# Layer 3's depthwise convolution: planes padded to nine columns, shifted copies made by the loads, taps split by the vector engine

## What is computed

```python
def _L3_conv_ref(x, w, b):
    xp = jnp.pad(x, ((0, 0), (0, 0), (3, 3), (3, 3)), mode='reflect')
    out = jax.lax.conv_general_dilated(xp, w, window_strides=(1, 1), padding='VALID',
              dimension_numbers=('NCHW', 'OIHW', 'NCHW'), feature_group_count=192)
    return out + b[None, :, None, None]
...
x = x + _L3_conv_ref(_gn(x), L3_conv_w, L3_conv_b)
```

## Time and profile before

| | us |
|---|---|
| median of 3 runs | 2519.12 (2515.17 to 2522.4) |
| profiled execution | 2517.25 |
| its span, first to last instruction | 2515.5 |
| TensorE busy | 1945.1 (77%) |
| VectorE busy | 1287.4 (51%) |
| ScalarE busy | 804.7 (32%) |
| POOL busy | 870.2 (35%) |
| layer 3's block, from its first normalisation to the end | 2316.3 to 2515.5 |

### The profile page before, as it was taken

How to read it: one execution, slowest core, us unless ns; L and a number is a source line. 1 busy time by engine, 2 the same in 40 slices (tenths; PEclk the granted TensorE clock), 3 DMA queues, 4 the chain that set the end, 5 groups by cost and what they waited for, 6 DMA issues and landing times. The chain is left out here.

```text
span 2515.5 us, 36893 instructions
## 1 busy us (share of the span) xinstructions
PE 1945.1 (77%) x15660; PEld 1203.3 (48%) x15660; DVE 1287.4 (51%) x1313; ACT 804.7 (32%) x1269; POOL 870.2 (35%) x459
## 2 busy tenths in 40 slices
PE   3879779769999999999978768777777777774052
PEld 1577666667777777777734322222222222221031
DVE  6445444441111111111271166799999999988803
ACT  3445445440000000000122125633543533335410
POOL 3334233220000000000000040599899899983300
PEclk9889899889999999999988778899899979987555
DMA  7899999988131313130120040678688868863799
GB/s 197 249 311 314 316 292 304 296 257 241 59 118 59 118 60 118 60 118 1 43 59 11 0 139 21 156 197 219 171 213 216 209 175 213 218 179 90 224 215 294
DMA packets 195538, 424.51 MB, mean 169 GB/s; under 512 B 18733, under 2 KB 143661, under 8 KB 184717
## 3 DMA queue, kind: packets, MB, share of 16 engines
q1 hardware_dynamic: 182540, 414.81, 58.8%
q10 hardware_dynamic: 12832, 7.34, 1.1%
HBM read 299.33 MB, written 121.96 MB: 167 GB/s over the span
## 5 line engine op out<-in xcount | busy, mean ns | idle before, releaser
L743 PE MATMUL ps<-mem 128*128 128x288 f16 x5376 | 654.6, 287 | 14.4 <-DMA mem<-depthwise_out 14.4
L743 PEld LDWEIGHTS ps<-mem 128*128 128x128 f16 x5376 | 502.1, 98 | 152.9 <-issue 15.4
L1717 POOL TENSOR_TENSOR mem<-mem 128x1024 f32<-128x1024 f32 x192 | 465.7, 2444 | 45.3 <-ACT mem L1651 42.9
L1626 PE MATMUL ps<-mem 128*128 128x512 f32 x768 | 417.9, 676 | 39.1 <-POOL mem L1717 35.0
L1112 POOL TENSOR_TENSOR mem<-mem 128x1536 f16<-128x1536 f32 x16 | 50.8, 3180 | 940.3 <-ACT mem L1090 940.3
L533 PE MATMUL ps<-mem 56*96 56x240 f16 (+1 forms) x5184 | 308.2, 280 | 86.1 <-DMA mem<-base_phases 53.0
L533 PEld LDWEIGHTS ps<-mem 56*96 56x96 f16 x5184 | 297.7, 128 | 111.4 <-DMA mem<-base_phases 58.5
L786 DVE TENSOR_TENSOR mem<-ps,mem 128x128 f16<-128x128 f32 x64 | 18.7, 292 | 586.8 <-ACT mem L807 586.8
L1746 DVE TENSOR_TENSOR_SCAN mem<-mem,ps 128x1024 f32<-128x1024 f32 x132 | 307.8, 2332 | 18.2 <-issue 10.3
L646 DVE TENSOR_TENSOR mem<-ps,mem 96x1024 f16<-96x1024 f32 x144 | 175.3, 1220 | 217.9 <-ACT mem L578 217.9
L1626 PEld LDWEIGHTS ps<-mem 128*128 128x128 f32 x768 | 153.5, 213 | 242.9 <-issue 134.5
(11 more groups left out here) (202 smaller groups left out, 1915.4 us busy)
## 6 DMA issues: line engine op xcount, KB each, us to landing
mem<-l_bc SPq DMA_DIRECT2D x504, 256.0 KB, 4.5
depthwise_out<-mem SPq DMA_DIRECT2D x105, 512.0 KB, 9.4
mem<-depthwise_out SPq DMA_DIRECT2D x31, 1664.0 KB, 10.8
mem<-base_phases SPq DMA_DIRECT2D x72, 448.0 KB
base_phases<-mem SPq DMA_DIRECT2D x56, 512.0 KB, 9.9
mem<-in_wd SPq DMA_DIRECT2D x72, 336.0 KB
mem<-l_planes SPq DMA_DIRECT2D x48, 252.0 KB
mem<-in_x SPq DMA_DIRECT2D x4, 2048.0 KB, 13.6
```

The lines of the kernel that those rows point to most:

```text
L743: ins = nc.tensor.matmul(ps[:, 2 * (i % 2) + h, 0:HALF], d, pw[rows, wa, k, HALF * h:HALF * h + HALF], start=(k == 0 and n == 0), stop=(k ...
L1626: ins = nc.tensor.matmul(py[:, a, :], ident, hh[:, n % 4, 512 * a:512 * a + 512], start=(n % N == 0), stop=(n % N == N - 1))
L1717: nc.gpsimd.tensor_tensor(hh[:, n % 4, :], hh[:, n % 4, :], cs[:, n % 4, :], ALU.mult).then_inc(hc_pool, 1)
```

## The change

- A plane becomes 18 rows of 9 blocks and 2 elements more (164). The ninth column lies between the end of one row and the start of the next, so the phases that are shifted by one block are the same data one element further on. SBUF and DRAM hold only the 32 phases; the copies L1952 and L2013 go.
- A half window is loaded by three transfers (`load_windows`): 32 phases, then 12 rows of them one element later and 12 one element earlier. `planes_d` has the phase outermost, so a row of a half window is one run of 10.5 KB, and a tile is stored in pieces of 656 bytes. SP loads the halves t = 0, ACT the halves t = 1.
- Six column copies stay, into the ninth column; the mirrored rows are copied in twelve pieces; the values that nothing writes are cleared first (`clear`), and POOL clears one element at each end of a window.
- The taps' low parts are made by DVE: piece 0 after tile 1, pieces 1 to 3 after tile 2. `w32` and `win` no longer share memory. TensorE waits for piece n // 3 before batch n.
- SP loads windows 0 to 2 after the store of tile 1 and ahead of that of tile 2.

```diff
-PLANE = 18 * 8
+PLANE = 18 * 9 + 2
...
-        planes_d = nc.dram_tensor("l3_planes", [B, C, TAPROWS, 2 * PLANE], F16).ap()
+        planes_d = nc.dram_tensor("l3_planes", [PHASES, C, B, 2 * PLANE], F16).ap()
...
-    pl = ar.take16(2, TAPROWS * 2 * PLANE, dt=F16)
-    cv = pl.rearrange("p a n -> p (a n)").bitcast(F32)[:, 0:NT * HW].rearrange("p (t n) -> p t n", t=NT)
-    pl = pl.rearrange("p a (c r h n) -> p a c r h n", r=4, h=2, n=PLANE)
+    shared = ar.take(NT * HW)
+    cv = shared.rearrange("p (t n) -> p t n", t=NT)
+    pl = shared[:, 0:PHASES * 2 * PLANE].bitcast(F16).rearrange("p (a f r h n) -> p a f r h n", a=2, f=8, r=4, h=2)
     wh = ar.take16(2, NB3 * WC, dt=F16)
-    at = ar.at
     win = ar.take16(NW, BP, PITCH, dt=F16)
-    end = ar.at
-    ar.at = at
     w32 = [ar.take(3 * WC) for _ in range(2)]
...
-        return pl[:, t % 2, 0:8, r, a, 8:136]
+        return pl[:, t % 2, :, r, a, 0:18 * 9].rearrange("p f (y x) -> p f y x", x=9)[:, :, 1:17, 1:9]
...
+    def load_windows(eng, n, t):
+
+        last, c0 = BP * PITCH, CB * n + BP * t
+        src = planes_d[:, c0:c0 + BP].rearrange("f c b n -> f (c b n)")
+        dst = win[64 * t:64 * t + TAPROWS, n % NW].rearrange("f c n -> f (c n)")
+        eng.dma_start(dst[0:32], src).then_inc(win_in[n % NW], 16)
+        eng.dma_start(dst[32:44, 1:last], src[20:32, 0:last - 1]).then_inc(win_in[n % NW], 16)
+        eng.dma_start(dst[44:56, 0:last - 1], src[0:12, 1:last]).then_inc(win_in[n % NW], 16)
...
                     load_taps(sp, t + 2)
                 sp.wait_ge(rows_done, t + 1)
                 for p0, b, c0, n in pieces(t):
-                    sp.dma_start(planes_d[b, c0:c0 + n].rearrange("c f n -> c (f n)"),
-                                 pl[p0:p0 + n, t % 2].rearrange("p c r h n -> p (c r h n)")).then_inc(stored[t], 16)
-            sp.wait_ge(tap_hi, NPIECE)
-            sp.wait_ge(tap_lo, NPIECE)
-            sp.wait_ge(stored[0], used + 16)
-            sp.wait_ge(stored[1], used + 16)
-            for n in range(NB3):
-                if n >= NW:
-                    sp.wait_ge(conv_sum, n - NW + 1)
+                    sp.dma_start(planes_d[:, c0:c0 + n, b].rearrange("f c n -> c f n"),
+                                 pl[p0:p0 + n, t % 2].rearrange("p f r h n -> p (f r) (h n)")).then_inc(stored[t], 16)
+                if t == 1:
+                    sp.wait_ge(win_cleared, 2)
+                    sp.wait_ge(stored[0], used + 16)
+                    sp.wait_ge(stored[1], used + 16)
+                    for n in range(NW):
+                        load_windows(sp, n, 0)
+            for n in range(NW, NB3):
+                sp.wait_ge(conv_sum, n - NW + 1)
                 if CB * n == 128:
                     sp.wait_ge(stored[2], used + 32)
-                for t in range(2):
-                    for b in range(B):
-                        c0 = CB * n + BP * t
-                        sp.dma_start(win[64 * t:64 * t + TAPROWS, n % NW, :, 2 * PLANE * b:2 * PLANE * b + 2 * PLANE],
-                                     planes_d[b, c0:c0 + BP].rearrange("c f n -> f c n")).then_inc(win_in[n % NW], 16)
+                load_windows(sp, n, 0)
...
-                pe.wait_ge(win_in[n % NW], win_base[n % NW] + 64 * (n // NW + 1))
-                if n == 0:
-                    pe.wait_ge(tap_hi, NPIECE)
-                    pe.wait_ge(tap_lo, NPIECE)
+                pe.wait_ge(win_in[n % NW], win_base[n % NW] + 96 * (n // NW + 1))
+                if n % 3 == 0:
+                    pe.wait_ge(tap_hi, n // 3 + 1)
+                    pe.wait_ge(tap_lo, n // 3 + 1)
...
+                                    out = ps[M3 * j:M3 * j + M3, bank(n) + t, 256 * h:256 * h + 256].rearrange("p (b y x) -> p b y x", b=B, x=8)
+                                    ins = nc.tensor.matmul(out, taps_of(n, 4 * h + j, o, t, a), x[:, :, xa, 9 * o:9 * o + 144].rearrange("p b (y x) -> p b y x", x=9)[:, :, :, 1:9],
...
-            def shift_right(t):
-                k = t % 2
-                act.wait_ge(x_lo, 4 * (t + 1))
-                nc.scalar.copy(grid(pl[:, k, 8:11])[:, :, :, 1:8], grid(pl[:, k, 5:8])[:, :, :, 0:7]).then_inc(shifted, 1)
-
             normalise(0)
             taps(0)
-            for t in range(NT):
-                shift_right(t)
-                if t + 1 < NT:
-                    normalise(t + 1)
-                taps(t + 1)
+            normalise(1)
+            taps(1)
+            normalise(2)
+            act.wait_ge(win_cleared, 2)
+            act.wait_ge(stored[0], used + 16)
+            act.wait_ge(stored[1], used + 16)
+            for n in range(NW):
+                load_windows(act, n, 1)
+            taps(2)
+            taps(3)
+            act.wait_ge(x_lo, 4 * NT)
...
+                if n + NW < NB3:
+                    if CB * (n + NW) == 128:
+                        act.wait_ge(stored[2], used + 32)
+                    load_windows(act, n + NW, 1)
...
-            def taps(i):
-                pool.wait_ge(tap_hi, i + 1)
-                s = slice(3 * WC * i, 3 * WC * (i + 1))
-                q = slice(0, 64 + TAPROWS)
-                nc.gpsimd.tensor_tensor(wh[q, 1, s], w32[i % 2][q], wh[q, 0, s], ALU.subtract).then_inc(tap_lo, 1)
-
-            for i in range(NPIECE):
-                taps(i)
+            edge = win.rearrange("p a c n -> p a (c n)")
+            nc.gpsimd.memset(edge[:, :, 0:1], 0.0).then_inc(win_cleared, 1)
+            nc.gpsimd.memset(edge[:, :, BP * PITCH - 1:BP * PITCH], 0.0).then_inc(win_cleared, 1)
...
+            def pads(t):
+
+                def at(f, n):
+                    return pl[:, t % 2, f, :, :, n:n + 144].rearrange("p r h (y x) -> p r h y x", x=9)[:, :, :, :, 0]
+
+                for i in (1, 2, 3):
+                    V.tensor_copy(at(8 - i, 9), at(i, 10)).then_inc(columns, 1)
+                for i in (0, 1, 2):
+                    V.tensor_copy(at(i, 18), at(6 - i, 17)).then_inc(columns, 1)
...
-                k = t % 2
-                dve.wait_ge(shifted, 2 * (t + 1))
+                p = pl[:, t % 2]
                 dve.wait_ge(columns, 6 * (t + 1))
                 for r in range(1, 4):
-                    V.tensor_copy(pl[:, k, :, r, :, 0:8], pl[:, k, :, 4 - r, :, 8:16])
+                    V.tensor_copy(p[:, 3:8, r, :, 0:9], p[:, 3:8, 4 - r, :, 9:18])
+                    V.tensor_copy(p[:, 0:3, r, :, 1:10], p[:, 0:3, 4 - r, :, 10:19])
                 for r in range(3):
-                    ins = V.tensor_copy(pl[:, k, :, r, :, 136:144], pl[:, k, :, 2 - r, :, 128:136])
+                    V.tensor_copy(p[:, 3:8, r, :, 153:162], p[:, 3:8, 2 - r, :, 144:153])
+                    ins = V.tensor_copy(p[:, 0:3, r, :, 154:163], p[:, 0:3, 2 - r, :, 145:154])
                 ins.then_inc(rows_done, 1)
 
-            for k in range(2):
-                V.memset(pl[:, k, :, 0, :, 0:8], 0.0).then_inc(zeroed, 1)
-                V.memset(pl[:, k, :, 3, :, 136:144], 0.0).then_inc(zeroed, 1)
+            def taps(i):
+                dve.wait_ge(tap_hi, i + 1)
+                s, q = slice(3 * WC * i, 3 * WC * (i + 1)), slice(0, 64 + TAPROWS)
+                V.tensor_tensor(wh[q, 1, s], w32[i % 2][q], wh[q, 0, s], ALU.subtract).then_inc(tap_lo, 1)
+
+            def clear(k):
+
+                p = pl[:, k].rearrange("p f r h n -> p (f r h) n")
+                V.memset(p[:, :, 0:162].rearrange("p g (y x) -> p g y x", x=9)[:, :, :, 0:1], 0.0).then_inc(zeroed, 1)
+                V.memset(p[:, :, 162:164], 0.0).then_inc(zeroed, 1)
+                V.memset(pl[:, k, :, 0, :, 1:9], 0.0).then_inc(zeroed, 1)
+                V.memset(pl[:, k, :, 3, :, 154:162], 0.0).then_inc(zeroed, 1)
+
+            clear(0)
+            clear(1)
+            dve.wait_ge(zeroed, 8)
             for t in range(NT):
-                k = t % 2
                 if t == 2:
                     dve.wait_ge(stored[0], used + 16)
                 for r in range(4):
                     dve.wait_ge(x_norm, 4 * t + r + 1)
-                    V.tensor_copy(main_rows(t, r, 0), phase_rows(r)).then_inc(x_hi, 1)
+                    V.tensor_copy(main_rows(t, r, 0), flat(phase_rows(r))).then_inc(x_hi, 1)
                     dve.wait_ge(x_hi, 4 * t + r + 1)
-                    V.tensor_tensor(main_rows(t, r, 1), phase_rows(r), main_rows(t, r, 0), ALU.subtract).then_inc(x_lo, 1)
+                    V.tensor_tensor(main_rows(t, r, 1), flat(phase_rows(r)), main_rows(t, r, 0), ALU.subtract).then_inc(x_lo, 1)
                 dve.wait_ge(x_lo, 4 * t + 4)
-                V.tensor_copy(grid(pl[:, k, 11:14])[:, :, :, 0:7], grid(pl[:, k, 0:3])[:, :, :, 1:8]).then_inc(shifted, 1)
-                for i in range(3):
-                    V.tensor_copy(column(k, 8 + i, 0), column(k, 3 - i, 0)).then_inc(columns, 1)
-                    V.tensor_copy(column(k, 11 + i, 7), column(k, 6 - i, 7)).then_inc(columns, 1)
+                pads(t)
                 rows(t)
+                if t == 1:
```

(4 more changed lines are left out.)

11 lines of the change are left out of this document (2 added, 9 removed).

## The result

The changed kernel takes **2555.45 us** (median of 4 runs, 2551.64 to 2568.42), the kernel before 2519.40 beside it: the ratio is **1.0142**, with an interval of 1.0121 to 1.0164. It is 36 us slower. The forecast was 2511 with a range of 2497 to 2529, and 0.23 for slower.

A forecast was written before the change was run, and what follows sets the result against it. It took plane building, then window loads (6.5 us a batch) and instruction packets (5.94 us a burst) as bounds. TensorE would end at 2474 instead of 2481.6, -7.6 us: span 2508, median 2511, range 2497 to 2529.

The forecast's parts named there:

- Start of layer 3: ScalarE's first normalising step, taken at 2316.3 us as in the kernel before.
- Clearing: Eight VectorE memsets ahead of tile 0: 2.9 us, 0.8 of it seen, as VectorE waits for its first row anyway.
- Planes and casts: VectorE building planes: cast stays at 0.69 us, twelve row copies at 0.11 each; tile 1 done at 2341.3, not 2351.0.
- The stores' wait: SyncE's stores wait for taps' low parts: store 0 at 2344.4, store 1 at 2374, windows at 2389 instead of 2374.
- Stores: Plane stores in 656-byte pieces at 42 ns: 10.8 us each, plus 1 to 2 for completion and 3.3 for taps.
- Rival C: Plane stores: 656-byte pieces are slow, 62 to 65 ns each, giving 2527 us; chance 0.18.
- First windows: First window loads issued at 2389, 0.5 issue + 2 + 4.7 us; TensorE starts at 2396, 5 us earlier.
- The gap before batch 3: Store 2, 10.8 us, ahead of batch 3's half window in SyncE's queue: TensorE idles 5 us, batch 3 at 2420.
- Steady state: Last nine batches at 6.0 us each, from 2420 to 2474; windows and stores 6.6 at most, instruction packets 4.1 to 6.7.
- Tail: From last matmul to the end, eviction, store, load, add and output store: 33.9 us, as before.
- Rival D: Window halves don't overlap on two queues: 221 GB/s, 7.2 us a batch, 2522 us (2525 with slow first group); chance 0.15.

The follow-up runs named there:

- e16: e12 with SyncE's loads of the convolution's sums issued only after ScalarE's half of the last window load; 2498.71 us, ratio 0.9906.
- e10: The changed kernel, clearing only pads that nothing writes later (256 single elements a buffer instead of 1152); 2554.10 us.
- e17: The same kernel as e10, run again with five rounds; 2547.96 us, ratio 1.0097.
- e1: The changed kernel with SyncE's load of taps t + 2 issued after store t + 1 instead of ahead of store t; 2519.34 us, ratio 0.9996.
- e4: The changed kernel with the taps' low parts made by GpSimd again, SyncE's order as in the change; 2520.76 us, ratio 0.9999.
- e2: The changed kernel with all window loads in SyncE's queue, none in ScalarE's; 2555.18 us, ratio 1.0138.
- e3: The changed kernel with the eight clearing memsets made by GpSimd instead of VectorE; 2555.91 us, ratio 1.0144.
- e12: e5 with store 2 issued by GpSimd instead of SyncE; 2505.20 us, ratio 0.9937.
- e14: The same kernel as e5, run again with five rounds; 2510.56 us, ratio 0.9956.
- e9: e5 without the two 12-row loads of a half window from the fourth batch on (sums not valid); 2488.00 us, ratio 0.9866.
- e5: The changed kernel with small clearing and mended order: early stores ahead of tap loads, windows ahead of store 2, taps copied earlier; 2506.33 us, ratio 0.9939.
- e6: e5 with store 2 issued ahead of SyncE's first window loads instead of behind them; 2512.47 us, ratio 0.9954.

## Why the prediction was wrong

The wait that makes the kernel slower was named; what the forecast set against it did not come. It had 85 us from the first window's issue to the last matmul (2389 to 2474), where the kernel before takes 107.7. Measured: 119.8 (2402.0 to 2521.8). The windows, store 2 and the stored sums of that stretch are some 23 MB, so 85 us would have needed about 270 GB/s (an estimate from the sizes of the transfers); the two stretches above that cover most of it show 224 and 233, and the quickest kernel of the study, e16, took 96 us for it. **That is the step that failed: each transfer was priced by itself.** Store 2 was 10.8 us, a batch 6.0 where its own two terms made 6.6, and the sums that the first batches store beside store 2 were left out. By the steps of the prediction, against the profiled execution (span forecast 2508, measured 2554.5):

- **Start of layer 3:** +1.4 us, chance.
- **Clearing (wrong, +7.2):** put at 2.9 us, of which 0.8 seen, from a memset of 768 f32 elements. That row is of contiguous elements. 1152 single ones take 5.1 to 5.2 us, twice; e10 and e17 show 7.6 us of it ahead of store 0.
- **Planes and casts (right):** the cast stays at 0.69, also with runs of 8 at a pitch of 9, as the rule of the Trainium skill quoted there has it (VectorE: DVE Perf Modes, "What auto-detection actually checks"); row copies 0.1 each. A batch of matmuls that read with the pitch of 9 takes 3.6 to 4.0 us where its row stands whole, 4.04 before, so taking nothing for the pitch was right.
- **The stores' wait (right):** store 0 was forecast at 2344.4 and came at 2353.0, which is the two terms above; store 1 at 2374, came at 2384.4; VectorE idle for "some 16 us", 18.25. e1 and e4 show from both ends that this wait is the cause. e1 also shows what the order alone is worth: 36 us. The prediction gave no such price; its 15 (windows 2389 instead of 2374, measured 28 later) are against the kernel before, with the gains of the planes in them.
- **Stores (+4.3):** 656-byte pieces at 42 ns; measured 37. But a store landed 17.5 to 17.8 us after its issue, forecast 15 to 16. Rival C (slow pieces) falls.
- **First windows (+3.7):** 7 us from issue to TensorE, measured 10.6.
- **The gap before batch 3, the fourth as the prediction counts from 0 (wrong, +15.6 up to there):** 10.8 us of store 2 in SyncE's queue was forecast to end in 5 us of idling, batch 3 starting 24 us after batch 0. The queue was held for 20.2 + 13.2 us, the gap was 22.3, and batch 3 started 39.6 us after batch 0. In these 39.6 us the engines were busy for 0.98 and moved 8.9 MB: store 2, six halves of windows and six stores of sums went through them together. In e2, e3, e10 and e17, which have the same order, it was 35.6 to 39.6 us. That the held queue makes the gap isn't shown (e12, e14).
- **Steady state (wrong, +15.7):** 6.0 us a batch. The prediction's own sum, 4.7 for the windows and 1.9 for the stored sums, made 6.6, and it took off 0.6 for overlap. No overlap showed: eight batches took 6.8 us each (2452.2 to 2506.7, +6.6) with the engines busy for 0.89, which before had 6.7, and e9 shows that the transferred bytes set this pace. The ninth took 15.1 (+9.1), for the sums' loads in front of the last half window (e16).
- **Tail:** 32.7, forecast 33.9.

1.4 + 7.2 + 4.3 + 3.7 + 15.6 + 15.7 - 1.2 is 46.7 of the 46.5 us. These are differences of one profiled execution, and the gap alone varied by 7 us between e5 and e14. Rival D was nearest in kind (7.2 us a batch, no gain from two queues) but had the time at 2522, since it had the early steps of the forecast.

Before, 45.8 MB moved in the 180.5 us behind store 0, 254 GB/s; in e1 43.5 MB in 178 us, 244 GB/s. So the change saves 5% of the bytes, and e1 shows no better rate. But the rate is no constant: from store 0 to the end e14 moves the same bytes at 260 GB/s and e16 at 268. What differs most is how long the engines idle. Taken from the DMA shares, which are rough, it is about 32 us of 202 in the change, 14 of 178 in e1, 5 of 167.5 in e14, 6 of 162 in e16. Of the 36 us between the change and e1, 13.5 are store 0's later start and about 18 this idle time.

What the runs leave open: why rows of 10.5 KB into 56 partitions are no faster per byte than 576-byte pieces were, while the engines reach some 400 GB/s when the sums are loaded; why the single elements cost 4.5 ns; the remaining gap of 11 to 13 us before the fourth batch in e12 and e16, and why it was 19.0 and 11.8 us in the same kernel; and what store 2 in GpSimd's queue is worth once the last batch waits no longer (e16 changes both against e14).

## What to carry to other kernels

When work moves from one engine to another, look for every wait on its semaphore in all queues: a load that waited for an early result can become the cork in front of a store, in a line that the diff doesn't show. Where the DMA engines are nearly full, first sum the bytes of the whole stretch and see which rate the forecast needs; then look for the time in which the engines idle, and for large loads that overtake what the next step waits for. Here an order that made the engines idle cost 36 us, an overtaking load made the last batch wait 11 us, and no gain from a second queue showed. Read an idle time that ends in "issue" ahead of a short row as part of that row's cost until a run shows otherwise. Profile the same kernel twice before a gap in one profile is read as an effect.

## What was not expected of the hardware

- A memset of 1152 single f16 elements at a stride of 9 takes 5.1 us on VectorE (its row shows 1.02 behind 4.08 of "issue" where another memset ended just before) and 5.20 on GpSimd: 4.5 ns an element, against 0.9 for contiguous f32. With 256 elements (e5) the same pair is 0.86 + 0.27 us.
- A one-source cast of VectorE took 9.52 us beside ten GpSimd memsets, which read nothing, and 0.70 without them (e3 and the change).
- The two halves of store 2, 4096 pieces together, held SyncE's queue for 16 to 20 us where they were issued behind window loads (6 in e6, ahead of them), and the load behind them for another 6 to 15. GpSimd issued the same store in 2.36 us (e12).
